# A two-layer decoder on one core: attention scores as three fp16 products, and the additions into X shared among three engines

## The reference

```
qkv = jnp.einsum('bsh,hf->bsf', x, w_qkv)            # x: the layer norm of x
scores = jnp.einsum('bhqd,bhkd->bhqk', q, k) / jnp.sqrt(jnp.float32(D_HEAD))
probs = jax.nn.softmax(scores, axis=-1)
values = jnp.einsum('bhqk,bhkd->bhkd', probs, v)      # q is summed: a scale of v
out = jnp.einsum('bsf,fh->bsh', values, w_o)
```

## Time and profile before

| | us |
|---|---|
| median of 3 runs | 1038.68 |
| lowest, highest | 1034.64, 1038.96 |
| the profiled execution, its own time | 1033.97 |
| span of the profiled execution | 1032.2 |
| granted TensorE clock over the span | 0.952 |

### The profile page before, as it was taken

The page is one execution under the profiler, slowest core; times in us unless marked ns, Lnnn a source line. Parts: engine busy times, 40 slices in busy tenths (PEclk is TensorE's granted clock), DMA queues, the critical chain, the costliest instruction groups (busy, mean ns, idle before and its releaser), DMA issues. The chain is left out here.

```text
span 1032.2 us, 18827 instructions
## 1 busy us (share of the span) xinstructions
PE 935.7 (91%) x6676; PEld 704.7 (68%) x6676; DVE 736.6 (71%) x1845; ACT 506.9 (49%) x1219; POOL 340.1 (33%) x341
## 2 busy tenths in 40 slices
PE   4786899999999999999998699999977699999976
PEld 2454677777777777777776498787754598786843
DVE  4643778888787888878776536877688427787786
ACT  1442565666556565665555422534347223534455
POOL 4003355554545555554554301510010302510000
PEclk9898899999999999999999899999899699999998
DMA  7313111110011111001000000000000000000001
GB/s 244 89 16 109 32 32 31 31 31 3 27 31 31 31 31 31 7 24 31 10 6 1 1 1 1 1 2 1 1 1 21 23 1 1 2 1 1 1 1 41
DMA packets 34432, 25.18 MB, mean 24 GB/s; under 512 B 9332, under 2 KB 31436, under 8 KB 34380
## 3 DMA queue, kind: packets, MB, share of 16 engines
q1 hardware_dynamic: 34380, 24.50, 9.0%
HBM read 22.32 MB, written 2.17 MB: 24 GB/s over the span
## 5 line engine op out<-in xcount | busy, mean ns | idle before, releaser
L452 POOL CAST exp_hi<-exp_scores 128x1024 f16<-128x1024 f32 x64 | 67.2, 1051 | 230.7 <-ACT exp_scores L545 230.7
L545 ACT ACTIVATE exp_scores<-banks,exp_bias,unscale 128x256 f32<-128x256 f32 x256 | 140.9, 560 | 2.1
L73 PE MATMUL banks<-value_out_hi,xn_t_hi 128*128 128x256 f16 x512 | 139.9, 273 | 2.3 <-DVE X L793 2.3
L1168 POOL TENSOR_TENSOR rstd_stream<-rstd_stream,neg_half 128x2 f32<-128x2 f32 x40 | 31.6, 789 | 331.2 <-DVE rstd_stream L1310 295.6
L74 PE MATMUL banks<-value_out_lo,xn_t_hi 128*128 128x256 f16 x512 | 139.8, 273 | 0.0
L75 PE MATMUL banks<-value_out_hi,xn_t_lo 128*128 128x256 f16 x512 | 139.7, 273 | 0.0
L454 POOL TENSOR_TENSOR exp_lo<-exp_scores,exp_hi 128x1024 f16<-128x1024 f32 x64 | 137.2, 2144 | 5.1
L957 PE MATMUL banks<-qk 128*128 128x256 f32 x512 | 124.1, 386 | 11.1 <-ACT exp_scores L545 11.1
L957 PEld LDWEIGHTS banks<-qk 128*128 128x128 f32 x512 | 98.7, 194 | 32.3 <-issue 12.8
L793 DVE SCALAR_TENSOR_TENSOR X<-banks,colsum,X 128x256 f32<-128x256 f32 x256 | 106.2, 478 | 11.9 <-DVE colsum L784 11.2
L527 ACT ACTIVATE qk<-banks 128x512 f32<-128x512 f32 x128 | 76.1, 598 | 64.0 <-PE banks L75 64.0
(11 more groups left out here) (222 smaller groups left out, 2034.0 us busy)
## 6 DMA issues: line engine op xcount, KB each, us to landing
head_weights<-in_wqkv_d SPq DMA_DIRECT2D x32, 128.0 KB, 3.6
weight_absmax_rows<-across_partitions SPq DMA_DIRECT2D x16, 256.0 KB, 4.1
X<-in_x_d SPq DMA_DIRECT2D x4, 512.0 KB, 7.4
head_weights<-in_wqkvt_d SPq DMA_DIRECT2D x16, 128.0 KB, 3.3
head_weights<-in_w_o_d SPq DMA_DIRECT2D x16, 128.0 KB, 3.2
out<-x_stream SPq DMA_DIRECT2D x8, 256.0 KB, 2.1
features_then_ternary<-in_c_fc_d SPq DMA_DIRECT2D x1, 1024.0 KB, 5.1
features_then_ternary<-in_c_proj_d SPq DMA_DIRECT2D x1, 1024.0 KB, 9.1
```

Source lines behind the costliest of these rows:

```text
L73: nc.tensor.matmul(out, lhs[0], rhs[0], start=first, stop=False)
L452: nc.gpsimd.tensor_copy(probh[:, s1_.par], prob[:, s1_.par]).then_inc(exph_ready, 1)
L545: last = nc.scalar.activation(prob[:, s1_.par, t, :], sc_ps[t // ST][:, t % ST, :], ACT.Exp, bias=nbias[:, t:t + 1], scale=unscale[:, s1_. ...
```

## The change

The copies of q and k write fp16 high halves (ScalarE), and VectorE subtracts them from PSUM into fp16 low halves, ahead of the row maxima. TensorE makes each score product as three fp16 products, and waits for the low halves where it waited for the copies. Of the four additions into X of a step, VectorE keeps the two of bank 4. ScalarE scales the two tiles of bank 5 into an SBUF buffer `x_scaled`, at the end of its iteration, behind the exps, and GpSimd adds the buffer into X in one instruction of 128x512, at the end of its iteration.

```
--- before.py
+++ after.py
@@ -130,7 +130,8 @@
     stats = sb("ln_stats", [P, NT, 6])
     mv = sb("ln_mean_var", [P, NT, 2])
     rstd = sb("ln_rstd", [P, NT])
-    qk = sb("qk", [P, 2, 2, NPAIR])
+    qkh = sb("qk_hi", [P, 2, 2, NPAIR], F16)
+    qkl = sb("qk_lo", [P, 2, 2, NPAIR], F16)
     nmax = sb("neg_rowmax", [P, 2 * ST])
     nbias = sb("exp_bias", [P, TP])
     prob = sb("exp_scores", [P, 2, TP, S])
@@ -141,6 +142,7 @@
     rhl = sb("rowsum_inverse_halves", [P, 2, TP, 2], F16)
     csraw = sb("colsum_raw", [P, TP])
     csum = sb("colsum", [P, TP])
+    xscaled = sb("x_scaled", [P, ST, D])
 
     ctxt = sb("ctx_t", [P, KT, B * M])
     wk0 = sb("wk0_t", [P, KT, D])
@@ -221,7 +223,8 @@
     mhi_ready = sem("mhi_ready")
     mlo_ready = sem("mlo_ready")
     qk_full = sem("qk_full")
-    qk_ready = sem("qk_ready")
+    qkhi_ready = sem("qkhi_ready")
+    qklo_ready = sem("qklo_ready")
     sc_full = sem("scores_full")
     nmax_ready = sem("nmax_ready")
     nbias_ready = sem("nbias_ready")
@@ -234,7 +237,7 @@
     csraw_ready = sem("csraw_ready")
     csum_ready = sem("csum_ready")
     xm_full = sem("xm_full")
-    x_added = sem("x_added")
+    x_added, xm_scaled, x_pooled = sem("x_added"), sem("xm_scaled"), sem("x_pooled")
     pool_turn = sem("pool_turn")
     first_loads, second_loads, loads = sem("context_and_wk0_loaded"), sem("wv0_loaded"), sem("context_loads")
     k0_full, k0_ready = sem("k0_full"), sem("k0_ready")
@@ -456,8 +459,14 @@
                 pool.wait_ge(rrh_ready, i * 2)
                 nc.gpsimd.tensor_tensor(rhl[:, s1_.par, :, 1], rrow[:, s1_.par, :], rhl[:, s1_.par, :, 0],
                                         ALU.subtract).then_inc(rrl_ready, 1)
+            if runs(i, 2):
+                s2 = Step(i, c - 2)
+                pool.wait_ge(xm_scaled, i - 1)
+                mine = g.X[:, TP * s2.p + ST:TP * (s2.p + 1), :]
+                nc.gpsimd.tensor_tensor(mine, mine, xscaled[:, :, :], ALU.add).then_inc(x_pooled, 1)
 
         run(pool, step)
+        pool.wait_ge(x_pooled, STEPS)
 
     @block.scalar
     def _(act):
@@ -524,7 +533,7 @@
             if runs(i, 0):
                 for s in range(2):
                     act.wait_ge(qk_full, i * 2 + s + 1)
-                    nc.scalar.activation(qk[:, st.par, s, :], qk_ps[s], ACT.Copy).then_inc(qk_ready, 1)
+                    nc.scalar.activation(qkh[:, st.par, s, :], qk_ps[s], ACT.Copy).then_inc(qkhi_ready, 1)
             if later_head(i, c, 1):
                 act.wait_ge(m_full, h + 1)
                 value_out_hi(st.u)
@@ -546,6 +555,15 @@
                                                 bias=nbias[:, t:t + 1], scale=unscale[:, s1_.u, 0:1],
                                                 accum_out=rowsum[:, s1_.par, t:t + 1])
                 last.then_inc(exp_ready, 1)
+            if runs(i, 2):
+                act.wait_ge(csum_ready, i - 1)
+                act.wait_ge(xm_full, i * 2 - 2)
+                if not known(i) or i >= 3:
+                    act.wait_ge(x_pooled, i - 2)
+                for t in range(ST):
+                    last = nc.scalar.activation(xscaled[:, t, :], xm_ps[1][:, t, :], ACT.Copy,
+                                                scale=csum[:, ST + t:ST + t + 1])
+                last.then_inc(xm_scaled, 1)
             if known(i) and i == TERNARY + 3:
                 for n in range(2):
                     act.wait_ge(tern, 2)
@@ -767,6 +785,11 @@
             if preps(i, c, 3, 2):
                 dve.wait_ge(w_loaded[st.u], nth * 64 + 64)
                 absmax(st.u)
+            if runs(i, 0):
+                for s in range(2):
+                    dve.wait_ge(qkhi_ready, i * 2 + s + 1)
+                    nc.vector.tensor_tensor(qkl[:, st.par, s, :], qk_ps[s], qkh[:, st.par, s, :],
+                                            ALU.subtract).then_inc(qklo_ready, 1)
             if runs(i, 1):
                 dve.wait_ge(sc_full, i)
                 nc.vector.tensor_reduce(nmax[:, :], sc_both, AX.X, ALU.max, negate=True).then_inc(nmax_ready, 1)
@@ -781,17 +804,18 @@
                 nc.vector.tensor_scalar(csraw[:, :], halves[:, :, 1], unscale[:, s2.u, 1:2], None,
                                         ALU.mult).then_inc(csraw_ready, 1)
                 dve.wait_ge(csraw_ready, i - 1)
+                if not known(i) or i >= 3:
+                    dve.wait_ge(xm_scaled, i - 2)
                 nc.vector.scalar_tensor_tensor(out=csum[:, :], in0=halves[:, :, 0], scalar=unscale[:, s2.u, 1:2],
                                                in1=csraw[:, :], op0=ALU.mult, op1=ALU.add).then_inc(csum_ready, 1)
                 if not known(i) or i >= 3:
                     dve.wait_ge(x_added, i - 2)
                 dve.wait_ge(csum_ready, i - 1)
             if runs(i, 2):
-                for t in range(TP):
-                    if t % ST == 0:
-                        dve.wait_ge(xm_full, (i - 2) * 2 + t // ST + 1)
+                dve.wait_ge(xm_full, (i - 2) * 2 + 1)
+                for t in range(ST):
                     last = nc.vector.scalar_tensor_tensor(
-                        out=g.X[:, TP * s2.p + t, :], in0=xm_ps[t // ST][:, t % ST, :], scalar=csum[:, t:t + 1],
+                        out=g.X[:, TP * s2.p + t, :], in0=xm_ps[0][:, t, :], scalar=csum[:, t:t + 1],
                         in1=g.X[:, TP * s2.p + t, :], op0=ALU.mult, op1=ALU.add)
                 last.then_inc(x_added, 1)
             if not known(i):
@@ -939,7 +963,7 @@
                 cols = slice(NPAIR * st.p, NPAIR * (st.p + 1))
                 for s in range(2):
                     if not known(i) or i >= 1:
-                        pe.wait_ge(qk_ready, i * 2 - 1 + s)
+                        pe.wait_ge(qklo_ready, i * 2 - 1 + s)
                     for k in range(KT):
                         ws = slice(k * DH, (k + 1) * DH)
                         last = pair_matmuls(nc, qk_ps[s], (whi[:, st.u, s, ws], wlo[:, st.u, s, ws]),
@@ -947,23 +971,23 @@
                     last.then_inc(qk_full, 1)
             if runs(i, 1):
 
-                pe.wait_ge(qk_ready, i * 2)
+                pe.wait_ge(qklo_ready, i * 2)
                 if not known(i) or i >= 2:
                     pe.wait_ge(exp_ready, i - 1)
                 for b in range(2):
                     for t in range(ST):
                         q = slice(b * S + t * P, b * S + (t + 1) * P)
                         kk = slice(b * S, (b + 1) * S)
-                        last = nc.tensor.matmul(sc_ps[b][:, t, :], qk[:, s1_.par, 0, q], qk[:, s1_.par, 1, kk],
-                                                start=True, stop=True)
+                        last = pair_matmuls(nc, sc_ps[b][:, t, :], (qkh[:, s1_.par, 0, q], qkl[:, s1_.par, 0, q]),
+                                            (qkh[:, s1_.par, 1, kk], qkl[:, s1_.par, 1, kk]), True, True)
                 last.then_inc(sc_full, 1)
             if runs(i, 2):
 
                 if s2.p == 0:
                     pe.wait_ge(mlo_ready, h + 1)
-                if not known(i) or i >= 3:
-                    pe.wait_ge(x_added, i - 2)
                 for b in range(2):
+                    if not known(i) or i >= 3:
+                        pe.wait_ge((x_added, xm_scaled)[b], i - 2)
                     for t in range(ST):
                         rows = slice((TP * s2.p + b * ST + t) * P, (TP * s2.p + b * ST + t + 1) * P)
                         for k in range(KT):
```

## The result

The changed kernel takes **1067.54 us** (median of 4 runs, 1064.02 to 1073.59) against 1038.76 (4 runs, 1034.64 to 1038.96): a ratio of 1.029, 95% interval 1.023 to 1.035. It is slower. The prediction was 1065.0, range 1030 to 1082, with 0.80 on slower.

A forecast was written before the change was run, and what follows sets the result against it. The prediction took TensorE as the bound before and a chain through VectorE and ScalarE after: 6.8 + 8.0 + 10.0 + 7.1 = 31.9 a head against 30.0, +27 over 14 heads, less 1, so 1038.7 becomes 1065, range 1030 to 1082.

The forecast's parts named there:

- TensorE's work: Scores group in each step: 1.73 us falls to 1.31, so 30.0 to 28.3 a head, alone a gain of 23 us.
- its other signs: In the loop: TensorE waits 1 to 2 us for exps, ScalarE's bias over 3 in the second step, L596 about 2.0.
- Chain: Row maximum to row maximum through VectorE and ScalarE, four steps a head: 31.9 us against 30.0, +27 over 14 heads.
- Third step: The step with `scales`: L596 waits out `exp_lo`, then the addition holds L599 or L602 for 1.0; 10.0 us.
- Low half: VectorE's subtraction of 128x512 from PSUM, two a step: 0.61 each, bounds 0.5 and 0.7.
- Scaling pair: ScalarE's two scaled Copies of 128x256 in each step: 0.8 for the pair.
- Addition: GpSimd's one addition of 128x512 in each step: 1.15, taken from `head_weights_lo`.
- 1: Rival: TensorE stays the bound, L596 in the third step not held; 27.9 for the vector-scalar chain, 1016; chance 0.07.
- 2: Rival: the addition hides between VectorE's work, only L596 waits for `exp_lo`; 29.7 a head, 1035; chance 0.12.
- 3: Rival: TensorE's clock falls too, to 0.88 in the loop; some 33.5 a head, 1089; chance 0.08.
- the last steps: After the loop, steps without a level part: they give some 1 us back, turning +27 into +26.
- the start: The steps before the loop: the prediction's sum had no term for them, and said no DMA is added or moved.

The follow-up runs named there:

- Experiment 2: The changed kernel with GpSimd adding only one of 256 columns of each scaled tile, place and waits kept: 1060.09, ratio 1.018, a head 31.10.
- scores_only_freed: Changed kernel with all X additions on VectorE, scale computation freed, L614 dropped, `value_out_lo` and `head_weights_lo` moved later: 1029.87, ratio 0.991; again 1029.11, 0.988.
- x_split_only: The changed kernel with scores kept in fp32, only the X additions split over the engines: 1043.25, ratio 1.005, a head 30.63.
- freed versions: Kernels with `weight_scale`'s factor on ScalarE, `unscale` behind the row maximum and L614 left out, some with further moves: 1024.63 to 1044.50.
- scales_freed: The changed kernel with `weight_scale`'s factor on ScalarE, `unscale` behind the row maximum and L614 left out: 1044.50, ratio 1.007, a head 30.38.

## Why the prediction was right, and where it was off

- **TensorE's work.** 1.66 less a head, from 30.0 to 28.3. Over the loop its busy time fell by 1.1, from 30.15 to 29.07 a head. The scores group takes 1.30 (415.33 to 416.63), as assumed. Half a microsecond of the difference is how busy time counts, an estimate: it takes in the last product before each gap to its end, 0.27 where the next could start after 0.11, and a head now has three to four gaps, 3.1 us in all. TensorE was busy for 90.3% of the loop, where the prediction had asked for less than 90; its other signs came, among them TensorE's wait for the exps (1.62 before a group of scores at 425.27) and ScalarE's wait of 3.09 for the row maximum in the second step. This part was a gain that the chain took back.
- **Chain.** Predicted 6.8, 8.0, 10.0, 7.1 for the first to fourth step, sum 31.9. Measured, means over the loop: 7.35, 7.97, 9.94, 6.93, sum 32.19. Only the first is off by more than 0.2. The loop lost 28.4 against 26.6.
- **Third step.** L596 "waits out all of `exp_lo`": yes in 13 heads of 14, 2.00 in the mean of all. L599 or L602 held by the addition, charged 1.0: L599 (now L617), 1.28 in the mean, 1.15 more than before. Experiment 2 removed 1.00 of it, and the third step fell by 0.93.
- **Terms.** Low half 0.61 until the next: 0.60, 0.68 long. Scaling pair 0.8: 0.84 long, 0.71 until the next. Addition 1.15: 1.27, with fp32 instead of fp16 out. The prediction's estimate of 1.6 came from the rule of the Trainium skill (GPSIMD Engine Reference, "4.1 Engine selection") that two-input elementwise work takes about twice as long on GpSimd as on VectorE. Measured, 1.27 is 1.4 times the 0.88 of the pair that VectorE still does; but that pair reads PSUM and multiplies as well, and no run here has the same addition on VectorE, so the rule itself was not tested.
- **Rivals.** 1 needed L596 to run free, and it did so in one head of 14; 2 needed the addition to hold nothing, and in the other 13 L617 lasted 1.23 or 1.24. 3 needed a lower clock; the windows show 1.00.
- **The term mis-sized: the last steps, "give some 1 back".** They lost 3.6. By step, after against before: 7.90 and 6.04, 9.16 and 9.75, 10.10 and 7.25, 6.79 and 7.31; so most of it lies in the third of them. ScalarE's timelines, before and after:

```profile
550.80 0.30 ACT L541 ACTIVATE exp_bias<-neg_rowmax,unscale 128x4 f32<-128x4 f32 x1 [4.80 <-DVE neg_rowmax L772]
...
553.31 3.90 ACT L552 ACTIVATE features_then_ternary<-features_then_ternary,ternary_rec 128x2048 f32<-128x2048 f32 x2
557.10 1.08 ACT L527 ACTIVATE qk<-banks 128x512 f32<-128x512 f32 x2
558.05 0.31 ACT L541 ACTIVATE exp_bias<-neg_rowmax,unscale 128x4 f32<-128x4 f32 x1
```

```profile
583.91 0.30 ACT L550 ACTIVATE exp_bias<-neg_rowmax,unscale 128x4 f32<-128x4 f32 x1 [4.84 <-DVE neg_rowmax L795]
...
587.13 3.91 ACT L570 ACTIVATE features_then_ternary<-features_then_ternary,ternary_rec 128x2048 f32<-128x2048 f32 x2
590.92 1.10 ACT L536 ACTIVATE qk_hi<-banks 128x512 f16<-128x512 f32 x2
...
594.01 0.30 ACT L550 ACTIVATE exp_bias<-neg_rowmax,unscale 128x4 f32<-128x4 f32 x1 [2.00 <-DVE neg_rowmax L795]
```

Here ScalarE does work for the second part, 3.9 us ahead of the copies of q and k. Before, the next row maximum was ready when these ended, since it did not need them: 7.25 from bias to bias. After, low halves and maximum come behind them: 10.10. The prediction asked what leaves the last steps, not what else their engines do.
- **A term put at nothing: the start.** Up to the fourth step the kernel lost 3.4. In the first steps VectorE waits for a DMA, and this wait grew by 2.8, before and after:

```profile
83.89 0.42 DVE L687 TENSOR_REDUCE nf_max<-nf_max_rows 128x2 f32<-128x256 f32 x1 [10.17 <-DMA nf_max_rows<-across_partitions]
```

```profile
87.35 0.42 DVE L705 TENSOR_REDUCE nf_max<-nf_max_rows 128x2 f32<-128x256 f32 x1 [12.98 <-DMA nf_max_rows<-across_partitions]
```

Why the DMA came later was not traced.

That 1065.0 came so near 1067.5 is in part luck. What was forecast is the first part's loss, 26; in the traces it lost 36.7, of which the loop, the only stretch worked out term by term, has 28.4. The medians are only 28.8 apart, because the profiled execution of before lies below its median and that of after above. The second part, which none of the kernels changed, takes 447 to 460 us in the traces here. `scores_only_freed` and `scores_only_freed_again` are one kernel: their first parts up to the last `exp_bias` differ by 1.3 us, the rest by 9.2, with a granted clock of 0.911 and 0.925 in the second part. The mechanism is shown by the loop, not by the nearness of the total.

What stays open: why `x_split_only` still takes 0.46 a head more, with TensorE 0.24 of 58 us idle; how the 32 us of `scores_only_freed` divide among its three moves; and how much of the gain in all freed versions comes from leaving L614 out and how much from the order.

## What to carry to other kernels

When a change takes work from the engine that bounds a loop, write down the chain through the others, step by step and with every stall, before counting the gain: here a bound of 28.3 by load became 32.2 by the chain. Look for tiny VectorE operations that stand between two engines' handovers beside a long GpSimd operation; here they cost almost nothing while TensorE was full, and up to the rest of their neighbour's length once it was not. And take them out of the chain first: the same fp16 scores then gained 1% instead of costing 2.5%.

## What the runs showed of the hardware that I had not expected

- A one-input cast on GpSimd holds VectorE too: L761 0.48 free, 1.32 when the cast (1.13) began inside the level part. The prediction had reckoned with holds beside the subtractions and the addition alone. The rule of the Trainium skill (SBUF — State Buffer, "SBUF: two separate sides") has it so, for a VectorE operation with two SBUF inputs against any GpSimd operation that reads SBUF; the trace agrees.
- Held operations are many sizes: 128x2 (1.28 in the mean instead of 0.13), 128x4 (2.00), one element (L857 in the last steps, 2.08 instead of 0.15). Reciprocals and reductions out of SBUF were never held in the first part of any run here: the reciprocals of 128x4 last 0.14 to 0.18 inside a GpSimd operation as outside, and in `scales_freed` L618 lasts 0.18 beside `exp_lo`, L615 1.07 beside the cast.
- A hold moves with the order. In `scales_freed` the first level operation (L747) lasts 0.94 in the mean, against 0.62 for the same operation (L744) after.
